# Attention on one Trainium2 core: the value products of a key tile issued in two halves of the queries

## The reference, cut to what matters

```
qh = q.reshape(B, S, KV, G, D).transpose(0, 2, 3, 1, 4)     # B=4, S=512, KV=8, G=4, D=16
scores = jnp.einsum('bkgsd,bktd->bkgst', qh, kh) / scale
weights = jax.nn.softmax(scores, axis=-1)
out = jnp.einsum('bkgst,bktd->bkgsd', weights, vh)
```

## Time and profile before

| what | value |
|---|---|
| median of 3 runs | 1661.46 us (1660.38 to 1663.22) |
| the profiled execution | 1661.82 us, span of its instructions 1659.9 us |
| PE busy | 1567.9 us, 94% |
| DVE busy | 947.7 us, 57% |
| ACT busy | 715.4 us, 43% |
| POOL busy | 701.0 us, 42% |
| attention, about 500 to 903 us of the span | PE 384.4, DVE 337.2, ACT 304.4 us busy of 403 |
| TensorE's granted clock, mean | 0.98 |

### The profile page before, as it was taken

One profiled execution on the slowest core, in us unless ns is written; L12 is line 12 of the kernel. 1 busy time (PEld: TensorE's weight loads), 2 busy tenths in 40 slices (PEclk: granted clock), 3 DMA queues, 4 the chain that ended last, 5 costly groups with the idle time before them and its releaser, 6 DMA issues.

```text
span 1659.9 us, 24705 instructions
## 1 busy us (share of the span) xinstructions
PE 1567.9 (94%) x8251; PEld 1050.8 (63%) x8278; DVE 947.7 (57%) x1539; ACT 715.4 (43%) x1166; POOL 701.0 (42%) x479
## 2 busy tenths in 40 slices
PE   6879999999989999999998799999999999999998
PEld 4565657565653333434333788788788888788886
DVE  6998979797888898988884522222222222222221
ACT  5885645455546777767776211111111111111111
POOL 1224261534513125353464756561771170930064
PEclk9889999999999999999999999999999999999999
DMA  9189800000231455343531615322340231530088
GB/s 354 70 305 386 291 1 1 1 1 1 85 94 45 121 138 150 92 129 109 150 105 55 213 69 178 125 78 70 146 177 31 83 127 28 188 127 26 26 141 214
DMA packets 90946, 196.18 MB, mean 118 GB/s; under 512 B 7154, under 2 KB 9075, under 8 KB 90227
## 3 DMA queue, kind: packets, MB, share of 16 engines
q1 hardware_dynamic: 71746, 156.68, 28.3%
q0 software_dynamic: 7168, 17.04, 4.6%
q10 hardware_dynamic: 11952, 21.43, 3.9%
HBM read 113.28 MB, written 81.32 MB: 117 GB/s over the span
## 4 chain that ended last, share of the span: by engine, by line
PE 69%; DVE 15%; POOL 6%; ACT 3%; DMA 3%; issue 3%; another core or an unknown queue 0%; SPq 0%; POOLq 0%; DVEq 0%; ACTq 0%
PE psum L2962 11%; PE psum L2964 11%; PE psum L2963 11%; PE psum L2605 7%; PE psum L2816 6%; PE psum L2805 5%; DVE neg_max L2081 4%; POOL expert_weight_parts L1070 3%; PE psum L2650 3%; PE psum L2779 3%; PE psum L2620 2%; DMA w_of_even_expert<-in_L_ffn_w 2%; PE psum L2986 2%; POOL expert_weight_parts L1069 1%; DVE inner_rotated_t_second L1945 1%
## 5 line engine op out<-in xcount | busy, mean ns | idle before, releaser
L2081 DVE TENSOR_REDUCE neg_max<-psum 128x2 f32<-128x1024 f32 x248 | 291.9, 1220 | 43.1 <-PE psum L2779 40.8
L1440 ACT ACTIVATE probabilities<-psum 128x512 f32<-128x512 f32 x512 | 269.8, 604 | 82.0 <-PE psum L2805 77.8
L2223 DVE TENSOR_TENSOR expert_inner<-psum,expert_inner 128x512 f32<-128x512 f32 x78 | 53.9, 691 | 390.2 <-ACT expert_inner L1545 390.2
L2962 PE MATMUL psum<-expert_weight_parts,sorted_tokens_t_first 128*128 x624 | 251.3, 403 | 9.0 <-POOL expert_weight_parts L1070 5.3
L2963 PE MATMUL psum<-expert_weight_parts,sorted_tokens_t_first 128*128 x624 | 247.5, 397 | 0.0
L2964 PE MATMUL psum<-expert_weight_parts,sorted_tokens_t_second 128*128 x624 | 247.4, 396 | 0.0
L1545 ACT ACTIVATE expert_inner<-psum 128x512 f32<-128x512 f32 x78 | 46.6, 598 | 397.9 <-PE psum L2964 397.9
L2805 PE MATMUL psum<-query_rows,key_rows 50*128 50x512 f32 x512 | 183.0, 449 | 5.8 <-ACT probabilities L1440 2.1
L2779 PE MATMUL psum<-key_rows,query_rows 48*128 48x512 f32 x496 | 176.2, 483 | 7.1 <-DVE neg_max L2081 3.3
L2962 PEld LDWEIGHTS psum<-expert_weight_parts,sorted_tokens_t_first 128*128 128x128 f32 x624 | 118.2, 189 | 37.6 <-issue 11.0
L2816 PE MATMUL psum<-probabilities,value_and_one 128*32 128x512 f32 x1024 | 139.3, 617 | 1.5 <-ACT probabilities L1440 0.9
(11 more groups left out here) (316 smaller groups left out, 2972.9 us busy)
## 6 DMA issues: line engine op xcount, KB each, us to landing
sorted_x<-zero_rows SPq DMA_DIRECT2D x9, 3960.0 KB, 30.7
w_of_odd_expert<-in_L_ffn_w SPq DMA_DIRECT2D x8, 2048.0 KB
wo_of_expert<-in_L_ffn_wo SPq DMA_DIRECT2D x7, 2048.0 KB, 8.5
query_rows<-query_rows_of_units SPq DMA_DIRECT2D x64, 192.0 KB, 3.6
w_of_even_expert<-in_L_ffn_w SPq DMA_DIRECT2D x6, 2048.0 KB, 11.6
sorted_tokens<-sorted_x ACTq DMA_DIRECT2D x39, 264.0 KB, 2.7
sorted_y<-expert_out ACTq DMA_DIRECT2D x39, 256.0 KB, 2.1
query_rows_of_units<-dims_first SPq DMA_DIRECT2D x32, 256.0 KB
```

The costliest lines, as they stand in the source:

```text
L1440: nc.scalar.activation(prob[t % 2][:, i * SEQ:(i + 1) * SEQ], ring(("score", n)), ACT.Exp, scale=HD ** -0.5).then_inc(c_e, 1)
L2081: nc.vector.tensor_reduce(of_pair[:, p, st, :], ring(("max", (m, i))).rearrange("p (h n) -> p h n", h=2), AX.X, ALU.max, negate=True).then ...
L2223: nc.vector.tensor_tensor(h, bank[2 * half + 1], h, ALU.mult).then_inc(e_h, 1)
L2962: nc.tensor.matmul(out_bank, hi[:, cols], w_r[:, bass.ds(w_at, 512)], start=start, stop=False)
```

## The change

`attend(k)` becomes `attend(k, half)`. Each call multiplies only 256 of the 512 queries of each head (so again 8 matmuls, in two rounds of four, of 256 columns). Half 0 is issued after P1 and half 1 after P3. Half 0 carries the waits; only half 1 signals c_pv.

```diff
-            def attend(k):
+            def attend(k, half):
 
                 u, t = k // ST, k % ST
-                pe.wait_ge(c_e, 4 * k + 4)
-                if t == 0:
-                    pe.wait_ge(c_v, u + 1)
-                    pe.wait_ge(c_oe, u)
+                if half == 0:
+                    pe.wait_ge(c_e, 4 * k + 4)
+                    if t == 0:
+                        pe.wait_ge(c_v, u + 1)
+                        pe.wait_ge(c_oe, u)
+                queries = slice(half * SEQ // 2, (half + 1) * SEQ // 2)
                 for h in range(GROUP):
-                    last = nc.tensor.matmul(bank[7][32 * h:32 * h + 32, :], v_u[u % KVH][:, t * 32:(t + 1) * 32],
-                                            prob[t % 2][:, h * SEQ:(h + 1) * SEQ], start=(t == 0), stop=(t == ST - 1))
-                last.then_inc(c_pv, 1)
+                    of_head = prob[t % 2][:, h * SEQ:(h + 1) * SEQ]
+                    last = nc.tensor.matmul(bank[7][32 * h:32 * h + 32, queries], v_u[u % KVH][:, t * 32:(t + 1) * 32],
+                                            of_head[:, queries], start=(t == 0 and half == 0), stop=(t == ST - 1 and half == 1))
+                if half == 1:
+                    last.then_inc(c_pv, 1)
...
                         if u == -1:
                             unread(3)
-                    k = ST * u + t - 1
-                    if 0 <= k < ST * UNITS and (there(u) or t == 0):
-                        attend(k)
+                        if 0 <= k < ST * UNITS and (there(u) or t == 0):
+                            attend(k, p)
```

More of the change, by code:

```diff
@@ L2806, in score @@
                                  q_r[u % 4][rows, p * SEQ:(p + 1) * SEQ], start=True, stop=True).then_inc(c_s, 1)
-            def attend(k):
+            def attend(k, half):
                 u, t = k // ST, k % ST
-                pe.wait_ge(c_e, 4 * k + 4)
-                if t == 0:
-                    pe.wait_ge(c_v, u + 1)
-                    pe.wait_ge(c_oe, u)
-                for h in range(GROUP):
-                    last = nc.tensor.matmul(bank[7][32 * h:32 * h + 32, :], v_u[u % KVH][:, t * 32:(t + 1) * 32],
-                                            prob[t % 2][:, h * SEQ:(h + 1) * SEQ], start=(t == 0), stop=(t == ST - 1))
-                last.then_inc(c_pv, 1)
+                if half == 0:
[4 more added lines that the diff above has]
+                queries = slice(half * SEQ // 2, (half + 1) * SEQ // 2)
+                for h in range(GROUP):
+                    of_head = prob[t % 2][:, h * SEQ:(h + 1) * SEQ]
[3 more added lines that the diff above has]
+                    last.then_inc(c_pv, 1)
             def attention(u):
                 for t in range(ST):
+                    k = ST * u + t - 1
                     for p in range(2):
```

## The result

The changed kernel is slower: 1691.34 us in the median of five runs (1684.47 to 1703.73) against 1661.46, a ratio of 1.0181 with a 95% interval of 1.0139 to 1.0223. The forecast was 1664.5, the range 1654 to 1678. The runs scatter over 19 us, those of the kernel before over 4. Ratios here leave out runs more than 1.5% above the fastest of the same kernel; medians and ranges take in all runs. The profiled one took 1703.73 us with a span of 1701.9 and a mean granted clock of 0.958, where before it was 0.983.

The account below looks back on a forecast made before the run. In the attention no engine was full; PE, ACT and DVE waited on each other in a ring. Terms of +4.5 (units), -3.0 (router units), +1.0 (rest) and +0.6 (last two units) summed to +3.1: 1664.5 us, range 1654 to 1678.

Parts of the forecast that it names:

- The ring of the plain tile: In a plain tile PE, ACT and DVE wait on each other in a 2.61 us chain; halves give 2.48.
- A half at 0.57 us: One visit's 256-column value products on PE: first round 0.24 us, second 0.33, bounds 0.50 and 0.99.
- Rival B: A half costs more than its share because weight loads show, over 0.62 us: 1680 us, chance 0.20.
- Rival A: PE's switches between score pairs and value products are free: 1632 us, chance 0.05.
- The spaces ending in t = 1 and t = 2: Value products to next, ending in tile 1 or 2; PE waits for a reduction: 3.32 for 2.82 and 3.27 us.
- The last two units: Attention's last two units: no DVE wait, ACT near its own rate, the two last halves together: +0.6 us.
- price of a second visit: On PE, one visit to the value products costs about 0.28 us besides the columns; the change doubles visits.
- the +3.1 of the sum: All terms over the attention together: +3.1 us, 1664.9 for the profiled execution, given as 1664.5 on the median.
- The clock: TensorE's clock falls in the attention: no term of their own; half clock stood within a rest of +1.0 us.
- rival C: The clock falls less in the attention, up to 8 us: 1656 us, chance 0.17; one more fall +4, 0.06.
- A different clock in the attention: Sign of being wrong: a granted clock in the attention unlike the one before would point to rival C.

Follow-up runs that it names:

- e2: Changed kernel with both halves behind the fourth pair, one visit a tile: 1663.86 us, ratio 1.0008 to the kernel before.
- e3: Kernel before with the value products whole (512 columns) but behind the second pair: 1711.79 us, ratio 1.0298.
- e11: The changed kernel run again, nothing altered: 1683.92 us, ratio 1.0170 to the kernel before.
- e1: Changed kernel with 8 extra fp32 products in PE's 1.9 us wait in the attention's first tile: 1676.71 us, ratio 1.0117 to the kernel before.
- e8: Changed kernel with two repeats of the first score product in every tile of units 0 to 2: 1701.60 us, ratio 1.0201 to the kernel before.
- e6: Kernel before with 8 extra fp32 products in the attention's first tile: 1657.64 us, ratio 0.9972.
- e12: Kernel before with 8 extra fp32 products in the first tile, a repeat of e6 with more rounds: 1658.05 us, ratio 0.9987.
- e9: Changed kernel with six full-array fp32 products ahead of the first score of each tile in units 0 and 1: 1698.98 us, ratio 1.0252.
- e10: Changed kernel with two visits a tile in units 0 to 3 only, both halves behind the fourth pair elsewhere: 1672.20 us, ratio 1.0067.
- e5: Changed kernel with both halves behind the fourth pair in units 0 to 3, two visits a tile elsewhere: 1679.84 us, ratio 1.0087.
- e4: Changed kernel with two visits only in tiles t = 3 and 0, both halves behind the fourth pair in the others: 1670.85 us, ratio 1.0053.

## Why the prediction was wrong

- **The ring of the plain tile and its new length**: right. 2.48 us was forecast for 2.61, 2.45 to 2.48 came, PE without a wait for an exponential, ACT without its 0.55 us.
- **A half at 0.57 us**: right, 0.24 and 0.33. Rival B falls: no load shows in the short round, and kernel e2 shows halves costing nothing. Rival A falls too: the switches cost what the rows had, 0.32 to 0.33 us in front of a half and 0.34 for the first pair behind it. The two rules of the Trainium skill weighed there, both of the page "TensorE: Matmul & The Clock Gate", don't cover this. By "Architectural detail: the array is 16× 32×32, not 1× 128×128" the queue pulls loads ahead, but the loads of a pair behind value products start with its own matmul (644.29, for which the earlier trace rows have the matmul):

```profile
644.29 0.18 PEld L2805 LDWEIGHTS psum<-query_rows,key_rows 50*128 50x128 f32 x1 [0.84 <-issue]
```

By "The mechanism" of Part 3 loads overlap only with products in other row groups, but the second round, on all rows, follows the first by 0.24 us.
- **The spaces ending in t = 1 and t = 2, +0.50 and +0.05**: right, 3.31 and 3.32 us; e3 confirms the ring with no cover, 3.74 us forecast and 3.74 to 3.75 measured.
- **The last two units, +0.6**: too small. The value products from t = 0 of unit 30 to the last take 25.2 us (920.32 to 945.55) where they took 21.5 (880.57 to 902.09): +3.7. The forecast had ACT near its own rate there, so that PE had time to spare. It had not. The first row is of the kernel before, the second of the changed one:

```profile
880.57:902.09 21.52, 19.06 (x138) 7.61 (x137) 7.06 (x19) 18.37 (x38) 9.51 (x23) 1.00 0.14 52
920.32:945.55 25.23, 22.27 (x214) 9.73 (x214) 8.16 (x22) 19.72 (x39) 11.23 (x24) 1.00 0.12 45
```

PE's busy time grew by 3.2 us, its waits by 0.5. A tile there takes 2.24 us before and 2.57 after, with no wait in either:

```profile
888.55 1.06 PE L2816 MATMUL psum<-probabilities,value_and_one 128*32 128x512 f32 x8
...
890.79 1.06 PE L2816 MATMUL psum<-probabilities,value_and_one 128*32 128x512 f32 x8
```

```profile
929.86 0.64 PE L2819 MATMUL psum<-probabilities,value_and_one 128*32 128x256 f32 x8
...
932.43 0.64 PE L2819 MATMUL psum<-probabilities,value_and_one 128*32 128x256 f32 x8
```

The forecast's own price of a second visit, 0.28 us, over these nine spaces gives 2.5. So this term of the sum left out the switches. It is the one part at full clock that was mis-sized, and it is about the difference between the +3.1 of the sum and the 6 us found at equal clock.
- **The clock**: the step that failed. The sum took the falls over as they were, a term of nothing, and rival C let them cost up to 8 us less or, with a chance of 0.06, 4 us more. Both were priced from the falls of the kernel before, which end after 3 to 7 us. Nothing in its trace shows how long a fall lasts in another rhythm. The longest lasted 61 us in one trace of the changed kernel and 27 in another, and over nine runs the clock cost some 21 us more than before. Most of that is falls that last longer, not more falls: from the attention's start to its last value products e11 has four with 51 us in all, where the kernel before has four with 17. The changed kernel's first trace has seven with 109. Each low stretch in two-visit tiles also costs more (4.32 for 2.48 us) than in one-visit tiles (3.82 for 2.61). "A different clock in the attention" was among the signs of being wrong; its direction was the unlikely one of the two.

What is shown: the clock is where the time is (the traces of the changed kernel and e1, the line through nine runs, the full-clock spaces). A stay of 27 us or more at the low level stands in three traces, all with two visits a tile (the changed kernel, e11, e8), and in none of the five with one visit (before, e2, e3, e6, e12). But e1 and e9, with two visits and without the first fall, had none either (10 us at most), and behind the first fall the two rhythms overlap: 61 and 10 us in the changed kernel and 10 in e10 against 3, 7, 7 and 14 in before, e2, e3 and e5. With one trace for each run that isn't proof.

What stays open: what in the rhythm decides it. Not how many columns a product has (e2). More half-array products don't help (e8). Filling the full array (e9) is undecided. A rival that no run separates is the waits. The changed kernel and e3 both put value products between the second and the third pair, both uncover the waits for reductions, and their runs are equally low in clock (medians of 0.968), while e2 keeps the old waits and is at 0.978 to 0.984. At the transpose shown above PE waits 1.04 to 1.12 us in the changed kernel, e11, e1 and e3, and each has a fall there; before, e6, e10 and e12 wait 0.70 or 0.71 us there and have none (e2, with 0.71, has a short one). Waits can't be what holds the clock down within the 61 us, in which PE had none, but they may set how often it falls. A kernel with two visits and the old waits was not run.

## What to carry to other kernels

A long product that runs behind the last of a ring's items can be the cover of another engine's wait elsewhere: before cutting it, follow the waits of every kind of tile, not of the common one. Where PE has no wait to give back, each extra change of kind is paid in full (0.33 us a tile in the last units). A forecast made from durations at full clock should ask separately how the clock behaves: list the waits in front of each fall in the trace of before, see which of them the change makes longer, and allow for a longer stay at the low level, since one run's profile doesn't show how it varies. Filling PE's 1.9 us wait at the start of the attention with idle products gave the kernel before 0.1 to 0.3%; with the halves of e4 it gave nothing.

## What the runs showed of the hardware

- TensorE can be busy by the profile for 61 us on end (61.00 of 61.00) and stay at 1.2 GHz. I had expected a busy PE to be back within some us, as in the kernel before.
- Two repeats of a product that fills 50 of 128 rows, in each of twelve tiles, did not bring it back: the clock was at 0.50 for 68 us.
- A change between these products and the fp32 value products costs about 0.1 us on either side, at both sizes. With 512 columns the last round takes 0.54 us and the first 0.45; with 256 columns they take 0.33 and 0.24. The first pair behind takes 0.34 instead of 0.24. Loads inside each kind are hidden.
- A fall is not the same in two executions of one kernel: behind the same 1.9 us wait the clock was low for 61 us in one trace of the changed kernel and for 10 in the other.
- One run of kernel e10 took 2177.82 us at a mean clock of 0.651, another 1723.46 at 0.883. By the conversion above, an estimate, the core was at 1.2 GHz for some 1500 us of the first. I have no cause for either.
